# Score groups given in two halves, and the orders of all engines laid out anew, in a fused attention and feed-forward kernel

## The reference

```python
xn = layernorm(x)
x = x + attention(xn, W_q, W_k, W_v, b_q, b_k, b_v) + ffn(xn, Wqkv, ...)

def ffn(x, ...):                       # 6 layers
    for i in range(6):
        x = attn_layer(shift_tokens(x), Wqkv[i], q_scale[i], k_scale[i], Wo[i]) + x
        x = ffn_layer(shift_tokens(x), ln_g[i], ln_b[i], W1[i], b1[i], W2[i], b2[i]) + x

def attn_layer(x, Wqkv, qs, ksc, Wo):  # 16 heads of 64
    q, k, v = split(x @ Wqkv)
    q, k = l2norm(q) * qs, l2norm(k) * ksc
    q, k = rotary(q), rotary(k)        # with the scales of xpos
    # windows of 32 queries, each sees its own and the last window, masked
    p = softmax(8 * q @ k.T + mask)
    return concat_heads(p @ v) @ Wo

def ffn_layer(x, g, b, W1, b1, W2, b2):
    a, gate = split((layernorm(x) * g + b) @ W1 + b1)
    return a * gelu(gate) @ W2 + b2
```

## Time and profile before

| | |
|---|---|
| median of 3 runs | 1632.88 us (1631.48 to 1635.65) |
| the profiled execution's own time | 1638.37 us |
| its span, first to last instruction | 1636.2 us |
| busy share of the span: PE, PEld, DVE, ACT, POOL | 92%, 79%, 83%, 85%, 76% |
| mean granted TensorE clock | 0.987 of full speed |
| DMA packets | 91,725, 79.83 MB |

### The profile page before, as it was taken

The page is one execution under the profiler, slowest core; times in us unless marked ns, Lnnn a source line. Parts: engine busy times, 40 slices in busy tenths (PEclk is TensorE's granted clock), DMA queues, the critical chain, the costliest instruction groups (busy, mean ns, idle before and its releaser), DMA issues.

```text
span 1636.2 us, 66314 instructions
## 1 busy us (share of the span) xinstructions
PE 1510.4 (92%) x26320; PEld 1300.5 (79%) x26320; DVE 1362.6 (83%) x2362; ACT 1393.7 (85%) x2646; POOL 1250.8 (76%) x1214
## 2 busy tenths in 40 slices
PE   5789999999999999999999999999999999999996
PEld 4678878888888878787878888887878888888885
DVE  5699888888888888888888888888888888889872
ACT  3578988899889889888988889898889888888986
POOL 5488878778887877787878778877878787777761
PEclk9899999999999999999999999999999999999997
DMA  5111111121121121121121121121112111111110
GB/s 144 46 41 48 45 31 46 33 83 45 34 64 38 45 73 45 32 68 35 45 77 40 33 64 48 36 66 48 46 33 69 43 37 40 36 45 34 48 46 22
DMA packets 91725, 79.83 MB, mean 49 GB/s; under 512 B 65690, under 2 KB 79006, under 8 KB 90654
## 3 DMA queue, kind: packets, MB, share of 16 engines
q1 hardware_dynamic: 90558, 75.34, 17.1%
q10 hardware_dynamic: 864, 0.26, 0.1%
HBM read 17.91 MB, written 1.05 MB: 12 GB/s over the span
## 4 chain that ended last, share of the span: by engine, by line
PE 64%; ACT 17%; issue 12%; DVE 5%; POOL 1%; DMA 0%; ACTq 0%; SPq 0%; DVEq 0%; POOLq 0%
PE bank L1064 53%; PE bank L1174 7%; ACT pz L680 4%; DVE parts L885 4%; PE bank L1209 3%; ACT sq L618 3%; ACT L607 2%; ACT L702 1%; ACT ot L687 1%; ACT gt L702 1%; ACT kt L642 1%; ACT es L672 1%; PE bank L1243 1%; ACT w_hi L591 0%; PE bank L1144 0%
## 5 line engine op out<-in xcount | busy, mean ns | idle before, releaser
L452 POOL TENSOR_TENSOR rot<-parts 128x512 f32<-128x512 f32 x384 | 491.9, 1287 | 133.4 <-DVE parts L885 131.0
L885 DVE TENSOR_TENSOR parts<-bank,rtab 128x1024 f32<-128x1024 f32 x384 | 459.2, 1207 | 118.2 <-ACT sq L618 118.1
L463 POOL TENSOR_TENSOR rot<-rot,rnorm 128x512 f32<-128x512 f32 x384 | 396.5, 1044 | 19.6 <-DVE rnorm L911 19.6
L469 POOL TENSOR_TENSOR es<-es,r 128x512 f32<-128x512 f32 x192 | 200.2, 1043 | 134.8 <-DVE r L937 134.8
L895 DVE TENSOR_REDUCE n<-sq 128x8 f32<-128x512 f32 x384 | 255.6, 678 | 33.9 <-ACT sq L618 32.7
L1064 PE MATMUL bank<-w_hi,x_hi 128*128 128x512 f32 x576 | 277.2, 481 | 2.9 <-DVE parts L885 1.8
L618 ACT ACTIVATE sq<-bank 128x512 f32<-128x512 f32 x384 | 229.1, 597 | 34.6 <-PE bank L1064 25.7
L1174 PE MATMUL bank<-ident,rot 128*128 128x128 f32 x1536 | 230.9, 273 | 4.6 <-POOL rot L463 3.9
L680 ACT ACTIVATE pz<-bank 64x512 f32<-64x512 f32 x384 | 226.3, 589 | 9.4 <-PE bank L1209 6.7
L1064 PE MATMUL bank<-w_lo,x_hi 128*128 128x512 f32 x576 | 229.9, 399 | 0.0
L1064 PE MATMUL bank<-w_hi,x_lo 128*128 128x512 f32 x576 | 229.3, 398 | 0.1
(11 more groups left out here) (87 smaller groups left out, 2817.1 us busy)
## 6 DMA issues: line engine op xcount, KB each, us to landing
vb<-v SPq DMA_DIRECT2D x96, 384.0 KB, 3.6
w_new<-in_Wqkv SPq DMA_DIRECT2D x6, 1536.0 KB, 8.2
vb<-v SPq DMA_DIRECT2D x48, 128.0 KB, 2.3
w_o<-in_Wo SPq DMA_DIRECT2D x6, 512.0 KB
xin<-x_tok SPq DMA_DIRECT2D x48, 64.0 KB, 2.5
xs<-x_tok SPq DMA_DIRECT2D x48, 64.0 KB, 2.1
xin<-x_tok SPq DMA_DIRECT2D x48, 56.0 KB, 2.9
xs<-x_tok SPq DMA_DIRECT2D x48, 56.0 KB, 2.1
```

Source lines behind the costliest of these rows:

```text
L452: g.tensor_tensor(rot[:, i * CH:(i + 1) * CH].rearrange(halves, z=2, c=HD), parts[:, b:b + CH].rearrange(halves, z=2, c=HD), parts[:, b + ...
L463: g.tensor_tensor(c, c, over(r, CHH, DH), ALU.mult).then_inc(s_sc[i], 1)
L469: g.tensor_tensor(e, e, over(r8[:, (u % 2) * PAIRS:(u % 2 + 1) * PAIRS], PAIRS, DH), ALU.mult)\
L885: d.tensor_tensor(parts[:, b:b + 2 * CH].rearrange("p (w h c) -> p w h c", w=2, c=DH), heads(bank[QK_BANK[i]][:, :]).unsqueeze(1).to_broad ...
```

## The change

- scores(n, T) now gives the masks and the first 64 of its 128 small matmuls, and a new function, other_scores(n, T), gives the other 64 and the signal s_s[T]. In TensorE's new order three products stand between the halves of group 0, and hidden, take_in, turn_normal, project_v and turn_p between those of group 1.
- The iterations of all five engines are put in new orders, and the banks are assigned anew. The orders were laid out with TensorE's instruction stream counted in blocks of 256.
- X is loaded by three transfers (sequence 0, sequences 1 and 2, the other 5), and moments and powers are taken for each part.
- Of the large memsets, vb, pz and ht are now VectorE's, before and after the first moments; kt, xin and xs are GpSimd's, at the very start. ScalarE runs one small Exp before the first attention, which loads its table. The casts of identity and mask come one sequence later.

The diff, cut:

```diff
-QK_BANK, T_BANK = (2, 5, 0, 2, 1, 3, 2, 3), (4, 1, 4, 1, 3, 4, 5, 0)
-V_BANK, P_BANK, O_BANK = (5, 2, 5, 2), (0, 0, 4, 1), (4, 0, 4, 0)
-S_BANK, W_BANK, H_BANK = ((6, 7), (6, 7)), (5, 5), (3, 3, 1)
-XIN_BANK, N_BANK, D_BANK = 4, 1, 2
-LAST_N2, LAST_SC = (3, 7), (3, 6)
+PARTS = ((0, 1), (1, 3), (3, SEQS))
+QK_BANK, T_BANK = (6, 5, 4, 2, 3, 4, 4, 3), (7, 7, 2, 0, 4, 7, 5, 0)
+V_BANK, P_BANK, O_BANK = (1, 1, 1, 4), (2, 0, 1, 3), (3, 2, 2, 0)
+S_BANK, W_BANK, H_BANK = ((6, 7), (7, 6)), (0, 5), (0, 5, 3)
+XIN_BANK, N_BANK, D_BANK = 0, 1, 4
+LAST_N2, LAST_SC = (3, 7), (0, 5)
...
-            sp.dma_start(tok[:, 1:], X4[:, 1:]).then_inc(s_x[1], 16)
+            for k, (a, b) in enumerate(PARTS):
+                if k:
+                    sp.dma_start(tok[:, a:b], X4[:, a:b]).then_inc(s_x[k], 16)
...
+            g.memset(kt[:, :], 0.0)
+            g.memset(xin[:, :], 0.0)
+            g.memset(xs[:, :], 0.0).then_inc(s_zero, 1)
...
+            a.activation(as2[:, :], ident[:, 0:TILES], ACT.Exp)
...
+            d.memset(vb[:, :], 0.0)
+
+            def first_moments(i):
+                a, b = TILES * PARTS[i][0], TILES * PARTS[i][1]
+                dve.wait_ge(s_x[i], 16)
+                for k in range(a, b):
+                    d.bn_stats(st0[:, k * 6:(k + 1) * 6], acc[:, k * P:(k + 1) * P]).then_inc(s_l0, 1)
+                dve.wait_ge(s_l0, a + b)
+                for k in range(a, b):
+                    d.bn_aggr(mv0[:, k * 2:(k + 1) * 2], st0[:, k * 6:(k + 1) * 6]).then_inc(s_l0, 1)
+
+            first_moments(0)
+            d.memset(pz[:, :], 0.0)
+            d.memset(ht[:, :], 1.0)
...
             dve.wait_ge(s_l0p, 1)
             first_normalise(0)
-            dve.wait_ge(s_l0, SEQS * TILES + TILES)
-            for k in range(TILES, SEQS * TILES):
-                d.bn_aggr(mv0[:, k * 2:(k + 1) * 2], st0[:, k * 6:(k + 1) * 6]).then_inc(s_l0, 1)
+            for i in range(1, len(PARTS)):
+                first_moments(i)
...
-                for half in range(PAIRS // 2):
+            def score_heads(n, T, halves):
+                for half in halves:
...
-                last.then_inc(s_s[T], 1)
+                return last
+
+            def scores(n, T):
...
+                score_heads(n, T, range(2))
+
+            def other_scores(n, T):
+                score_heads(n, T, range(2, PAIRS // 2)).then_inc(s_s[T], 1)
...
+                if live(n - 2):
+                    freed((s_rot[0], n - 1, 8, 0), (s_sub[1], n - 3, 4, 3))
+                    freed((s_qte[0], n - 2))
+                    scores(n - 2, 0)
+                if live(n - 1):
+                    freed((s_xready, n - 6), (s_rot[0], n - 2, 8, 6))
+                    project(n - 1, 2)
...
+                if live(n - 1):
+                    freed((s_v[3], n - 2), (s_rot[1], n - 1, 8, 5))
                     project(n - 1, 6)

```

More of the change, by code:

```diff
@@ L505, in iteration @@
                     add(n - 1, 4)
[L506 to L512, removed]
+                    add(n - 1, 5)
                 if live(n - 2):
@@ L707, in iteration @@
             def iteration(n):
+                if live(n - 2):
+                    first_root(n - 2, 1)
+                    half_square(n - 2, 1)
+                if live(n - 5):
+                    gelu(n - 5, 0)
+                if live(n - 2):
+                    copy_v(n - 2, 1)
+                if live(n - 1):
+                    square(n - 1, 1)
+                if live(n - 3):
+                    take_o(n - 3, 1)
                 if live(n - 1):
@@ L710, in iteration @@
                 if live(n - 3):
-                    take_p(n - 3, 3)
+                    take_o(n - 3, 0)
+                if live(n - 2):
+                    copy_v(n - 2, 0)
+                if live(n - 1):
+                    square(n - 1, 3)
+                if live(n - 2):
+                    take_qk(n - 2, 7)
+                if live(n - 3):
+                    take_p(n - 3, 2)
                 if live(n - 5):
@@ L714, in iteration @@
                     exp_and_log()
-                if live(n - 1):
-                    square(n - 1, 3)
+                if live(n - 2):
+                    take_qk(n - 2, 4)
+                if live(n - 3):
+                    take_p(n - 3, 3)
                 if live(n - 2):
                     exps(n - 2, 0)
+                    exps(n - 2, 1)
+                if live(n - 1):
+                    guard(n - 1, 0)
+                    square(n - 1, 4)
+                    square(n - 1, 5)
+                    logarithm(n - 1, 0)
+                if live(n - 2):
+                    take_qk(n - 2, 6)
+                    take_qk(n - 2, 5)
                 if live(n - 3):
@@ L721, in iteration @@
                 if live(n - 1):
[L722 to L727, removed]
+                    first_root(n - 1, 0)
+                    half_square(n - 1, 0)
+                if live(n - 3):
+                    take_o(n - 3, 3)
                 if live(n - 2):
                     copy_v(n - 2, 2)
[L730 to L739, removed]
+                if live(n - 5):
+                    gelu(n - 5, 2)
+                    exp_and_log()
                 if live(n):
@@ L742, in iteration @@
                 if live(n - 2):
-                    exps(n - 2, 1)
-                if live(n - 3):
-                    take_o(n - 3, 3)
+                    copy_v(n - 2, 3)
+                    take_p(n - 2, 0)
                 if live(n - 1):
                     next_hi(n - 1)
+                    square(n - 1, 6)
+                if live(n - 4):
+                    affine(n - 4)
                 if live(n - 2):
[L749 to L754, removed]
+                    take_p(n - 2, 1)
                 if live(n - 1):
-                    square(n - 1, 6)
-                    take_qk(n - 1, 1)
+                    square(n - 1, 7)
                 if live(n - 2):
@@ L760, in iteration @@
                 if live(n - 1):
[L761 to L765, removed]
+                    take_qk(n - 1, 1)
+                    take_qk(n - 1, 3)
                 if live(n):
@@ L768, in iteration @@
                 if live(n - 1):
[L769 to L773, removed]
                     guard(n - 1, 1)
[L775 to L778, removed]
                 if live(n - 2):
                     exps(n - 2, 3)
[L781 to L787, removed]
                 if live(n - 1):
-                    copy_v(n - 1, 1)
-                if live(n - 2):
-                    take_p(n - 2, 2)
+                    logarithm(n - 1, 1)
+                    take_qk(n - 1, 2)
+                    take_qk(n - 1, 0)
             for n in range(STEPS + DEEP):
@@ L974, in iteration @@
             def iteration(n):
+                if live(n - 2):
+                    newton_half(n - 2, 1)
+                if live(n - 3):
+                    reciprocals(n - 3, 2)
+                    sums(n - 3, 3)
+                if live(n - 2):
+                    newton_root(n - 2, 1)
+                if live(n - 1):
+                    rotate(n - 1, 1)
+                if live(n - 3):
+                    reciprocals(n - 3, 3)
                 if live(n - 1):
                     squares(n - 1, 1)
+                if live(n - 5):
+                    gated(n - 5, 0)
+                if live(n - 1):
+                    rotate(n - 1, 2)
                     squares(n - 1, 2)
+                    squares(n - 1, 3)
                 if live(n - 2):
+                    maxima(n - 2, 0)
+                if live(n - 4):
+                    stats(n - 4)
+                    moments(n - 4)
+                if live(n - 2):
+                    maxima(n - 2, 1)
                     less_max(n - 2, 0)
+                    less_max(n - 2, 1)
+                if live(n - 1):
+                    rotate(n - 1, 3)
                 if live(n - 5):
                     gated(n - 5, 1)
[L982 to L985, removed]
                 if live(n - 3):
@@ L995, in iteration @@
                 if live(n - 1):
[L996 to L1001, removed]
+                    rotate(n - 1, 5)
                     newton_half(n - 1, 0)
[L1003 to L1004 removed]
                 if live(n - 2):
                     sums(n - 2, 1)
[L1007 to L1010, removed]
                 if live(n - 1):
+                    newton_root(n - 1, 0)
                     squares(n - 1, 4)
@@ L1014, in iteration @@
                     reciprocals(n - 2, 1)
-                    less_max(n - 2, 2)
+                if live(n - 1):
+                    squares(n - 1, 5)
                 if live(n):
@@ L1019, in iteration @@
                     gated(n - 5, 2)
+                if live(n - 2):
+                    maxima(n - 2, 2)
+                    maxima(n - 2, 3)
+                    less_max(n - 2, 2)
+                    less_max(n - 2, 3)
                 if live(n - 1):
                     rotate(n - 1, 6)
+                    squares(n - 1, 6)
```

(11 more changed lines are left out.)

329 lines of the change are left out of this document (139 added, 190 removed).

## The result

The changed kernel takes 1662.11 us (median of 4, 1660.56 to 1666.81), the kernel before in the same rounds 1634.22. The ratio is 1.0178 (95% interval 1.0151 to 1.0204): slower by 1.8%, outside the forecast range and on the other side.

The account below looks back on a forecast made before the run. TensorE, busy 1308 of 1380 us, bounds the kernel, ScalarE close behind. Steps 37, start 8, fill and drain 7 us: 52 off the profiled 1638.4 gives 1586, or 1580 us as median; range 1540 to 1612.

Parts of the forecast that it names:

- the slower one: take_x behind the gelu table load holds VectorE, whose maxima come late for project(n,0); 1650 us, chance 0.08.
- DVE es: TensorE wait ahead of project(n,0), named as the sign that VectorE is held behind take_x; no size given.
- Fetch: Splitting score groups ends TensorE's waits for 256-instruction blocks, 1.46 us a step; 0.1 left (bounds 0 and 0.7).
- Rivals 2 and 3: 2: half the fetch waits stay, 1597 us, chance 0.13. 3: splitting doesn't end them, 1616 us, chance 0.06.
- ScalarE: project(6) waits for copy_v(3): ScalarE's stretch 14.6 us against TensorE's 13.5; 1.05 us a step (bounds 0 and 1.5).
- Rival 1: ScalarE keeps up, so no wait for copy_v; step 30.2 us, total 1536 us, chance 0.20.
- down and rotate 6: down comes later behind project(6), so TensorE's 0.62 us wait for VectorE's rotation product goes.
- TensorE's own step: TensorE's work without either old wait, 30.02 us, plus 0.1 for more changes between small and large matmuls: 30.1 us.
- Start: The second turn_x comes 8 us earlier through X in parts and moved memsets (3 to 11).
- Fill and drain: Outside the middle of the run, 7 of 8.2 us of "issue" waits go; the five-step depth is unchanged.
- The steps: A step of 30.1 + 0.1 + 1.05 = 31.25 us, 0.85 less than 32.10; 37 us over 43 iterations.

Follow-up runs that it names:

- a1_sp_later: The changed kernel with SP's later_weights, later_qkv and store calls moved two iterations later; 1591.27 us, ratio 0.9767 against the kernel before.
- the run with PARTS only: The kernel before with only X in three transfers, moments and powers by part, memsets where they were; 1625.11 us, measured once.

## Why the prediction was wrong

**The step that failed** is one sentence: "SP has every copy of v issued over 10 us before its values, and load_x almost a whole step before take_in." It holds in a usual step (copy_v0 at 320.12 for values at 346.85 us); in the eight long ones the copy was issued 1.9 to 3.9 us ahead. I placed SP's copies and loads against the other engines, found they stood two iterations earlier, and looked no further: the three calls whose *own* waits name a step were never placed, and the sum has nothing for them. They cost 71 us (54 the weight calls, 17 the stores), measured by moving them. Nor did I ask what is ahead of a copy among the transfers: behind the weights it landed after 5.6 to 9.3 us in place of some 3.4. No rival had SP in it; the slower one had VectorE behind ScalarE, for which nothing in the profile after speaks (its "DVE es" stands once, 0.9 us).

**With SP put right,** the run comes near the sum: forecast 1580, measured 1591 (a1_sp_later). That is 39 us less than the kernel before in the same rounds; I had 52. From profile to profile it is nearer: 1586 forecast, 1589.94 measured. The 5.5 us between the two forecasts were how far the profiled execution before stood above the median; this one stands 1.3 below its own. Span against span it is 48 us: 9 ahead of the first take_in, 1 from there to take_in(5), 29 in the 42 steps, 9 behind the last take_in. The terms:

- *Fetch.* The waits went, as forecast (0.1 us a step was to be left): "issue" 0.3 us in the changed kernel, 2 to 3 in the two quicker ones. Undoing the split brings 44.4 us back. The 1.46 us a step was the difference of two step lengths; the waits of the earlier trace rows themselves make 49.6 us in 43 steps, 1.15 each, and what the other 0.3 were is open. My reading of "issue" as the arrival of blocks of 256 is borne out by the places where the waits end; that the waits go with the split is shown twice. Rivals 2 and 3 fall.
- *ScalarE.* 1.05 us a step forecast, 1.06 measured. Both sums behind it were 0.3 to 0.4 us short, and their difference right: in ScalarE's timeline

```profile
321.28 0.60 ACT L640 ACTIVATE kt<-bank 128x512 f32<-128x512 f32 x1 [0.71 <-PE bank L1170]
...
331.98 1.28 ACT L700 ACT_TABLE_LOAD   x1
...
333.76 1.28 ACT L605 ACT_TABLE_LOAD   x1
...
335.33 0.59 ACT L627 ACTIVATE v<-bank 128x512 f32<-128x512 f32 x1
```

take_qk(7) starts at 321.28, copy_v(3) ends at 335.92 and project 6 starts at 335.98, 14.9 us after turn_qk(7) gave way to turn_p at 321.08; TensorE itself would have been there 1.03 us earlier. Taking the load at 333.76 out of the stretch took the whole wait away. Rival 1 had ScalarE keep up by itself, which it did not; the kernel with the load moved is in the state that this rival describes, and its 1536 us are near what that kernel measures (1542).
- *down and rotate 6.* The wait of 0.62 us is gone, as forecast.
- *TensorE's own step.* 30.1 forecast; 30.26 is the step once both waits are gone.
- *Start.* 8 forecast, 8.6 measured.
- *Fill and drain.* I had 7 us for them. In the changed kernel take_in(5) is 9.6 us earlier, 8.6 of which are the start, and the drain is 4.8 us longer. With SP put right the fill gives 1 and the drain 9 us (109.5 to 100.4), together more than the 8.2 us of "issue" waits outside the steps; where the rest comes from was not looked for.
- *The steps.* 31.44 us in the mean against 31.25; with 32.13 before, 0.69 us a step and not 0.85. That is some 8 us short.
- *The eight long steps* are longer than their wait: see the last section.

## What to carry to other kernels

When orders are laid out anew, place *every* call of *every* queue on one time axis, those without a place of their own in a step above all; a call that waits for another engine's late event blocks all transfers behind it, and its cost shows only on the steps where it does something. Look also at what it issues when it is let go: here large weights went out right ahead of the small copy that was already late. One long step in four was its mark here; look at the steps one by one, not at their mean. A split that costs nothing in work was worth 3% in the new order and 1% in the old one, but the new order brought a second chain (a table load between two points of TensorE) and gave back more in a queue that wasn't a suspect.

## What the runs showed of the hardware

The granted clock of TensorE fell after the wait for vb. The windows of that long step (us; busy time and count of PE, PEld, DVE, ACT, POOL; then the granted clock, DMA share, GB/s):

```profile
405.00:409.00 4.00, 4.00 (x35) 3.30 (x36) 3.71 (x8) 3.60 (x9) 2.25 (x3) 1.00 0.39 111
409.00:413.00 4.00, 0.78 (x28) 0.64 (x22) 0.74 (x2) 0.92 (x2) 3.69 (x4) 0.98 1.05 285
413.00:417.00 4.00, 3.27 (x104) 2.96 (x104) 0.57 (x1) 1.57 (x3) 0.00 (x0) 0.50 0.48 111
```

TensorE was busy 0.78 of the 4 us from 409 on; in the next 4 its clock was 0.50, the lower of its two levels (1.2 in place of 2.4 GHz). 32 matmuls of values took 1.98 us there and 1.10 in the usual step. So the 3.95 us wait made its step 6.7 us longer than 31.38.

All ten waits for vb of 3.1 us and more were followed by a stretch at 0.50; the three of 1.8 us, in the last layer and behind it, were not, and neither were those of 1.03. A length between does not settle it. In the kernel before an "issue" wait of 1.97 us ended at 213.00 us, and the next 4 us have a mean clock of 0.57:

```profile
209.00:213.00 4.00, 2.03 (x148) 1.75 (x143) 2.90 (x5) 3.40 (x6) 2.96 (x5) 1.00 0.16 36
213.00:217.00 4.00, 4.00 (x17) 3.05 (x18) 2.19 (x5) 1.70 (x2) 4.00 (x5) 0.57 0.36 103
```

One of 1.90 us that ended at 968.7 left it at 1.00. What decides between these was not tried.

VectorE's operations beside GpSimd's: x_tok of two tiles took 0.59 us alone, 1.88 beside GpSimd's tensor products, and 5.34 beside its memsets. In the run with PARTS only, the two tiles at 5.33 us met one memset (5.25 to 7.05 us) and took 1.87 us.
